# Attention in a fused sequence kernel: scores of two steps side by side, other products behind the sums, values a batch ahead, and selections on 64 partitions each

## The reference, cut to what matters

```python
qkv = x @ W_attn.T                       # 4 sets of queries, one of keys, one of values
for g in range(4):                       # query sets share keys and values
    att = einsum('bhqd,bhkd->bhqk', q_g, k) / sqrt(8)     # 16 heads of size 8, 256 tokens
    att = where(causal, att, -inf); att = softmax(att)
    outs.append(einsum('bhqk,bhkd->bhqd', att, v))
x = x + concatenate(outs) @ W_proj.T
```

## Time and profile before

| what | value |
|---|---|
| median of 3 runs | 786.8 us (785.27 to 787.71) |
| profiled execution, its own time | 785.32 us |
| its span, first to last instruction | 783.6 us |
| busy share of the span: PE, DVE, ACT, POOL | 93%, 87%, 86%, 72% |
| exponentials of attention, first and last start | 245.3 and 589.8 us |
| granted TensorE clock, mean | 0.995 |

### The profile page before, as it was taken

One profiled execution on the slowest core, in us unless ns is written; L12 is line 12 of the kernel. 1 busy time (PEld: TensorE's weight loads), 2 busy tenths in 40 slices (PEclk: granted clock), 3 DMA queues, 4 the chain that ended last, 5 costly groups with the idle time before them and its releaser, 6 DMA issues.

```text
span 783.6 us, 21138 instructions
## 1 busy us (share of the span) xinstructions
PE 730.7 (93%) x8042; PEld 410.2 (52%) x8042; DVE 678.6 (87%) x1958; ACT 671.6 (86%) x932; POOL 564.3 (72%) x622
## 2 busy tenths in 40 slices
PE   4798999999999899999999999999889999999996
PEld 3345667777776333333333333333325777677774
DVE  7998999899887878889989998878787889989885
ACT  5918999999998988888888888888976999899984
POOL 2898676665445999999999999999974445445542
PEclk9999999999999999999999999999999999999998
DMA  9210000000044244343444533554300000000000
GB/s 279 58 80 28 2 2 2 2 2 2 2 109 101 65 111 99 102 103 82 102 109 102 107 92 95 108 97 94 67 3 1 15 1 15 15 15 15 15 15 18
DMA packets 37964, 45.74 MB, mean 58 GB/s; under 512 B 6137, under 2 KB 23810, under 8 KB 37858
## 3 DMA queue, kind: packets, MB, share of 16 engines
q1 hardware_dynamic: 37858, 44.33, 23.0%
HBM read 27.53 MB, written 16.78 MB: 57 GB/s over the span
## 4 chain that ended last, share of the span: by engine, by line
PE 64%; DVE 18%; ACT 10%; issue 5%; POOL 2%; DMA 0%; ACTq 0%; DVEq 0%; POOLq 0%
PE psum L1379 15%; PE psum L1028 15%; PE psum L959 14%; PE psum L1307 7%; ACT prob L1314 6%; DVE mixed L1047 4%; PE psum L1447 4%; PE psum L1182 3%; ACT hidden_first L973 1%; ACT hidden_parts_first L975 1%; PE psum L698 1%; PE psum L1249 1%; DVE normed L394 1%; DVE stats L374 1%; DVE o_tok L1389 1%
## 5 line engine op out<-in xcount | busy, mean ns | idle before, releaser
L1314 ACT ACTIVATE prob<-psum 128x1280 f32<-128x1280 f32 x256 | 299.2, 1241 | 46.5 <-PE psum L1307 46.5
L1323 POOL TENSOR_SCALAR_AFFINE_SELECT prob<-prob 128x768 f32<-128x768 f32 (+1 forms) x384 | 311.3, 847 | 22.2 <-ACT prob L1314 20.6
L959 PE MATMUL psum<-xt_parts,w_parts 128*128 128x512 f16 x768 | 186.6, 379 | 0.0
L1379 PE MATMUL psum<-prob,vstack 128*32 128x512 f32 (+1 forms) x1536 | 167.0, 533 | 5.1 <-DVE o_tok L1389 2.2
L989 POOL TENSOR_TENSOR hidden_parts_second<-hidden_second,hidden_parts_second 128x512 f16<-128x512 f32 x64 | 77.6, 1213 | 94.8 <-ACT hidden_parts_second L975 94.8
L1047 DVE SCALAR_TENSOR_TENSOR mixed<-psum,comb_y,mixed 128x128 f32<-128x128 f32 x512 | 143.2, 340 | 1.6 <-PE psum L1028 1.5
L989 POOL TENSOR_TENSOR hidden_parts_first<-hidden_first,hidden_parts_first 128x512 f16<-128x512 f32 x64 | 79.2, 1238 | 73.0 <-ACT hidden_parts_first L975 73.0
L1307 PE MATMUL psum<-qstack,kstack 32*64 32x512 f16 (+1 forms) x1536 | 100.0, 362 | 14.8 <-ACT prob L1314 13.3
L959 PEld LDWEIGHTS psum<-xt_parts,w_parts 128*128 128x128 f16 x768 | 70.9, 98 | 65.0 <-issue 1.4
L973 ACT ACTIVATE hidden_second<-psum,b 128x512 f32<-128x512 f32 x128 | 88.4, 691 | 16.4 <-PE psum L959 14.9
L1028 PEld LDWEIGHTS psum<-w_parts,hidden_parts_first 128*128 128x128 f16 x1536 | 90.3, 98 | 19.6 <-issue 6.7
(11 more groups left out here) (155 smaller groups left out, 880.3 us busy)
## 6 DMA issues: line engine op xcount, KB each, us to landing
qstack<-qk_parts SPq DMA_DIRECT2D x128, 128.0 KB, 3.5
qk_parts<-parts SPq DMA_DIRECT2D x64, 192.0 KB, 3.2
kstack<-qk_parts SPq DMA_DIRECT2D x128, 32.0 KB, 3.5
stream<-u_folded SPq DMA_DIRECT2D x4, 512.0 KB, 7.8
kept_x<-stream SPq DMA_DIRECT2D x4, 512.0 KB, 2.7
out<-mixed SPq DMA_DIRECT2D x7, 256.0 KB, 2.3
w_whole<-L_ffn_W SPq DMA_DIRECT2D x1, 1024.0 KB, 9.0
taps<-c_taps SPq DMA_DIRECT2D x1, 640.0 KB, 6.9
```

What stands on the lines that cost most here:

```text
L959: last = e.matmul(bank(u % 4), m.w1[:, w_part, ex, cols], xt_parts[:, s, x_part, :], start=(n == 0), stop=(n == len(PRODUCTS) - 1))
L1314: e.activation(prob[:, n % PROBS, 0:COLS], psum[:, TILE * (n % 2):TILE * (n % 2) + COLS], ACT.Exp, scale=SCALE)\
L1323: return e.affine_select(kept, kept, [[0, n] for n in kept.shape[1:-1]] + [[sign, BLK]], ALU.is_ge, 0.0, base=BLK * half, channel_multipli ...
L1379: last = e.matmul(to[SLOT * lane:SLOT * (lane + 1)], vstack[:, b % 2, kind, c * LANES + lane].rearrange("p h r -> p (h r)"), weights_of(q, ...
```

## The change

- PE's order of a step becomes scores, sums, then what stands beside.
- The places beside move: queries and keys to 4, 11 and 15; the values of batch b+1 to step 7 of batch b; the projections to 7 and 15 (10 and 14 stay in the last batch). So two steps' scores stand next to each other wherever no sum and nothing beside is between them. Projections take the last 128 columns of bank 6, clear of the values' 384. The waits follow the new order of bank 6.
- Each selection takes its half's 64 partitions; both stand one behind the other at the step whose exponential they need, and the wait between them is gone (count `masked` goes by two per mask).
- POOL's reciprocal root moves from step 8 to step 6. It waits until the selections ahead of it are complete, and in step 7 the second selection waits until the root is complete.

```diff
 def tensor_at_x(e, b):
-        else:
-            e.wait_ge(v_copied, max(1, b - 1))
+        elif b == 3:
+            e.wait_ge(lo_done, 3 * b)
+        elif b > 3:
+            e.wait_ge(attn_done, HALVES * (b - 3))
+        else:
+            e.wait_ge(v_copied, 1)
 def tensor_qk(e, b, j):
-        elif j == 2 and b >= 3:
+        elif j == 1 and b == 2:
+            e.wait_ge(v_copied, b)
+        elif j == 1 and b > 2:
             e.wait_ge(attn_done, HALVES * (b - 3) + 1)
 def vector_qk_high(e, b, j):
+        elif j == 2 and b > 2:
+            e.wait_ge(projected, HALVES * (b - 2))
 def tensor_v(e, b):
-        elif b == 1:
-            e.wait_ge(lo_done, 3 * (b + 2))
+        elif b + 1 < BATCH:
+            e.wait_ge(lo_done, 3 * (b + 1) + 1)
         else:
-            e.wait_ge(attn_done, HALVES * (b - 1))
+            e.wait_ge(attn_done, HALVES * (b - 2))
 def vector_v(e, b):
         if b >= 2:
+            e.wait_ge(projected, HALVES * (b - 2) + 1)
             e.wait_ge(weighed, SUMS_B * (b - 1))
...
+    def mask_place(m, rows):          # as before, of the partitions in rows
+    def gpsimd_half_mask(e, m, half):
+        kept, sign = mask_place(m, slice(BLK * half, BLK * (half + 1))), 1 if half else -1
+        e.affine_select(kept, kept, [[0, n] for n in kept.shape[1:-1]] + [[sign, BLK]], ALU.is_ge, 0.0, base=0,
+                        channel_multiplier=-sign).then_inc(masked, 1)
     def gpsimd_mask(e, n):
         q, t = divmod(n, 4)
-        m = MASKS_Q * q
-        if t == 0:
-            gpsimd_second_half_mask(e, m)
-            if q:
-                gpsimd_first_half_mask(e, m - 1)
-        elif t == 1:
-            gpsimd_second_half_mask(e, m + 1)
-            gpsimd_first_half_mask(e, m)
-            gpsimd_first_half_mask(e, m + 1)
-        elif t == 3:
-            gpsimd_second_half_mask(e, m + 2)
+        if t != 2:
+            e.wait_ge(exped, n + 1)
+            gpsimd_half_mask(e, MASKS_Q * q + t - t // 2, 0)
+            if n == 0:
+                e.wait_ge(low_second, EXPERTS * FFN_CHUNKS)
+            elif n % STEPS_B == 7 and (root := root_of(n // STEPS_B)):
+                e.wait_ge(root[0].rstd, root[1] + 1)
+            gpsimd_half_mask(e, MASKS_Q * q + t - t // 2, 1)
...
+    QK_AT = (4, 11, 15)
+    def projects_at(b):
+        return (7, 15) if b + 1 < BATCH else (10, 14)
     def tensor_beside(e, b, at):
-        if b and at == 0:
-            tensor_v(e, b)
-        if b + 2 < BATCH and at in (4, 8, 12):
-            tensor_qk(e, b + 2, at // 4 - 1)
-        if b and at in (10, 14):
-            tensor_project(e, b - 1, at // 14)
+        if b + 2 < BATCH and at in QK_AT:
+            tensor_qk(e, b + 2, QK_AT.index(at))
+        if b + 1 < BATCH and at == 7:
+            tensor_v(e, b + 1)
+        if b and at in projects_at(b):
+            tensor_project(e, b - 1, projects_at(b).index(at))
         if b + 1 == BATCH and at == 2:
-            e.wait_ge(v_copied, BATCH)
+            e.wait_ge(attn_done, HALVES * (b - 1))
             tensor_xt(e, second, 0)
 def tensor_attention(e):
                 tensor_scores(e, n)
-            tensor_beside(e, *STARTS[n])
             if n >= 4:
                 for kind in (SUMS_Q if n < (BATCH - 2) * STEPS_B else SUMS_LAST)[n % 4]:
                     tensor_weigh(e, n // 4 - 1, kind)
+            tensor_beside(e, *STARTS[n])
 def gpsimd_attention(e):
-            if at == 8 and b % 2 == 0 and b // 2 + 2 < FFN_CHUNKS:
+            if at == 6 and root_of(b):
+                e.wait_ge(masked, HALVES * MASKS_Q * (n // 4) + HALVES * 2)
+            if at == 6 and b % 2 == 0 and b // 2 + 2 < FFN_CHUNKS:
                 gpsimd_mixed_rstd(e, b // 2 + 2)
```

More of the change, by code:

```diff
@@ L341, in build_in @@
     s_stack = [sem(f"stack_landed{i}") for i in range(2)]
-    scored, exped, half_masked, masked, weighed = (sem(n) for n in (
-        "scored", "exped", "second_half_masked", "masked", "weighed"))
+    scored, exped, masked, weighed = (sem(n) for n in (
+        "scored", "exped", "masked", "weighed"))
     turned, inverted_den, o_normed, rows_up, in_count, projected, attn_done = (sem(n) for n in (
@@ L1315, in scalar_exp @@
          .then_inc(exped, 1)
[L1319 to L1326, removed]
+    def mask_place(m, rows):
         q, t = divmod(m, MASKS_Q)
@@ L1329, in mask_place, with root_of @@
         if t < 2:
[L1330 to L1340, removed]
+            return prob[rows, slot].rearrange("p (n l g q) -> p n l g q", n=3, l=2, q=BLK)[:, :, 0]
+        return prob[rows, slot:slot + 2, 2 * BANK:COLS].rearrange("p n (g q) -> p n g q", q=BLK)
+    def gpsimd_half_mask(e, m, half):
+        kept, sign = mask_place(m, slice(BLK * half, BLK * (half + 1))), 1 if half else -1
+        e.affine_select(kept, kept, [[0, n] for n in kept.shape[1:-1]] + [[sign, BLK]], ALU.is_ge, 0.0, base=0,
+                        channel_multiplier=-sign).then_inc(masked, 1)
+    def root_of(b):
+        if b % 2 == 0 and b // 2 + 2 < FFN_CHUNKS:
+            return mixed_norm, b // 2 + 2
+        if b % 2 and b >= 3:
+            return expert_norm, second.at + (b - 3) // 2
     def gpsimd_mask(e, n):
         q, t = divmod(n, 4)
[L1345 to L1355 removed]
+        if t != 2:
[6 more added lines that the diff above has]
+            gpsimd_half_mask(e, MASKS_Q * q + t - t // 2, 1)
     def weights_of(q, kind, lane):
@@ L1426, in vector_bounds, with project_place @@
                                    op1=ALU.mult).then_inc(in_count, 1)
-    def project_bank(b):
-        return bank(6) if b + 1 < BATCH else bank(7)
+    def project_place(b, h):
+        if b + 1 == BATCH:
+            return bank(7)[:, h * P:(h + 1) * P]
+        return bank(6)[:, 3 * P:4 * P]
     def tensor_project(e, b, h):
         e.wait_ge(rows_up, HALVES * b + h + 1)
-        if b + 3 < BATCH:
-            e.wait_ge(lo_done, 3 * (b + 3) + h + 2)
+        if b + 3 < BATCH and h == 0:
+            e.wait_ge(lo_done, 3 * (b + 3) + 1)
+        elif b + 3 < BATCH:
+            e.wait_ge(lo_done, 3 * (b + 3) + 2)
         elif b + 3 == BATCH and h == 0:
-            e.wait_ge(v_copied, BATCH - 1)
+            e.wait_ge(attn_done, HALVES * b)
         elif b + 3 == BATCH:
@@ L1446, in tensor_project @@
         for g in range(SETS):
-            last = e.matmul(project_bank(b)[:, h * P:(h + 1) * P], o_rows[:, 1 - h, g, :], wproj[:, g, :],
+            last = e.matmul(project_place(b, h), o_rows[:, 1 - h, g, :], wproj[:, g, :],
                             start=(g == 0), stop=(g == SETS - 1))
@@ L1882, in vector_beside @@
     def vector_beside(e, b, at):
-        if b and at == 0:
-            vector_v(e, b)
         if b + 2 < BATCH and at == 2:
@@ L1887, in vector_beside @@
             vector_at_x_low(e, b + 2)
-        if b + 2 < BATCH and at in (4, 8, 12):
-            vector_qk_high(e, b + 2, at // 4 - 1)
-            vector_qk_low(e, b + 2, at // 4 - 1)
+        if b + 2 < BATCH and at in QK_AT:
+            vector_qk_high(e, b + 2, QK_AT.index(at))
+            vector_qk_low(e, b + 2, QK_AT.index(at))
+        if b + 1 < BATCH and at == 7:
+            vector_v(e, b + 1)
         if b and at == 5:
@@ L1894, in vector_beside @@
             vector_bounds(e, b // BOUNDED - 1, at // 13)
-        if b and at in (10, 14):
-            vector_attended(e, b - 1, at // 14)
+        if b and at in projects_at(b):
+            vector_attended(e, b - 1, projects_at(b).index(at))
         if b % 2 == 0 and b // 2 + 2 < FFN_CHUNKS:
```

10 lines of the change are left out of this document (5 added, 5 removed).

## The result

The changed kernel takes 804.9 us (median of 4 runs, 804.33 to 807.36), the kernel before, run beside it, 786.5 (785.27 to 787.71): a ratio of 1.0251, with a 95% interval of 1.0229 to 1.0273. I had forecast 778.4 with a range of 774 to 785, so it lies outside and on the other side. The profiled execution spans 805.6 us at a mean granted clock of 0.991; the run of 804.33 us had 0.995, the same as the profiled execution of the kernel before, so the clock is not what differs. Attention has taken the whole loss: from its first exponential to its last it is 362.4 us after and 344.5 before, 17.9 more.

The account below looks back on a forecast made before the run. In attention PE bounds the long quads, ACT's loop of 5.15 us the short ones. Thirteen batches gain 0.54 each (7.0), the last two 1.4: 8.4 off 785.3 gives 776.9, plus 1.5 for the median 778.4; range 774 to 785.

Parts of the forecast that it names:

- Selections: POOL's 24 mask selections a batch: no saving from half the partitions, 0.812 us each, so POOL needs 20.8 a batch.
- The slower rival: A selection on 64 partitions costs more than on 128, 5% more giving batches of 21.8 and 791 us; chance 0.10.
- Halves overlap: POOL takes both halves of a mask in the time of one, some 11 us a batch; 777 us, chance 0.15.
- The waits of POOL for itself: Two new waits on POOL, at the root and behind it: 0.15 us each, 0.3 a batch.
- Scores side by side: On PE, a pair of score blocks takes 0.52, saving 0.16; with work moved, a batch takes 20.74 us, 0.60 less.
- The neighbours forecast without a row: On PE, LATE followed by V or queries without scores between: taken as 0.57 us, give or take 0.16.
- the second quad: Steps 6 to 9 on PE, with V and a projection: 5.29 us, over the floor of 5.15.
- POOL is the bound: POOL needs 21.1 us a batch if self-waits cost 0.3 and the root's delay stays; 782.3 us, chance 0.20.
- DVE just fits: DVE's queue at step 7, 19.1 us a batch in all: LATE of step 11 ends 5.3 after step 7's, just enough.
- Waits and DMAs: nothing: SP's sends start some 4 us later, but the data is needed a whole batch (20.8) behind: no cost.
- The sum: Gain over attention: 13 batches x 0.54 = 7.0 us, batch 0 nothing, last two batches 1.4; in all 8.4.

Follow-up runs that it names:

- e11: e1 with the second selection of each quad's first mask cut to a third of its columns; 777.1 us, 0.9889 of the kernel before.
- e1: The changed kernel with POOL's part taken back (128 partitions, wait between a mask's two selections, root at step 8); 784.8 us, 0.9984 of the kernel before.
- e10: e1 with DVE's statistics in attention taken of only one tile in four; 784.8 us, 0.9976 of the kernel before.
- e7: e1 with DVE's statistics moved from step 1 to step 6 of each batch; 788.9 us, 1.0044 of the kernel before.
- the two probes: Two kernels, each executed once, of only groups of 16 POOL instructions, varying partitions, halves and operations; selections 0.86 us apart, 0.97 with halves in turn.

## Why the prediction was wrong

The step that failed is *Selections*: "So I take no saving and 0.812. The bounds are 0.41 ... and 0.85". In the changed kernel one takes 0.913, above the upper bound too, 0.10 over the value taken, and 24 of them make 2.4 us a batch. The question that I asked (what do fewer partitions cost?) I answered rightly: nothing, 0.86 on 128, 64 and 32. I didn't ask what it costs to go back and forth between them, since each row of before stands among neighbours on the same partitions. The price then went through by the prediction's own working, with 0.97 for the root in place of 1.3 for root and waits, in a queue that was already at 20.5 of 21.34: 22.9 a batch.

- *The slower rival* named the right place and the right sign of the outcome (24 selections pass 21.34 from 0.835 on), but for a cost of 64 partitions that doesn't exist, and at 5% where 12% came; 791 against 804.9. Its mark (a mean distance over 0.83) was the first thing to show.
- *Halves overlap* was wrong, and turned round: disjoint halves overlap less than equal ones.
- *The waits of POOL for itself*, put at 0.15 each, were too dear: the root and what follows it take 0.97 after and before, so the wait behind it costs nothing that can be seen; the one ahead of it is at most the 0.08 from the recorded end of the selection to the root.
- *Scores side by side* held. The neighbours forecast without a row measure LATE to V 0.57, V 0.73, projection 1.09, as taken; the pair ahead of the double sum takes 0.45, not 0.52, and by that alone the second quad is 5.22 and not 5.29. e11, with POOL relieved, has the quads 5.15, 5.22, 5.15, 5.15.
- *POOL is the bound* (782.3, chance 0.20) is the rival nearest to e1, the change without the halves: 784.8. I had let 20.80 stand since "those selections are done some 0.6 before LATE". e11 against e1 measures 7.8 us for relief on POOL. A reason can be argued and isn't shown: POOL was 20.5 of work in 21.34, a batch of 20.74 leaves it little slack to make up a delay, and batches that have one (up to 22.1) keep it. But e1's undisturbed batch of 21.15 loses its time at a wait for DVE and not for POOL.
- *DVE just fits* held for the time and not for the waits: with its work cut (e10) it is 784.8 as in e1, but in e1 the queries of step 4 wait for it, seven times and 3.5 us in all between 300 and 500 us, and the prediction had no wait there. It also took DVE's 19.1 us a batch as fixed, where e1 and e11 differ by 7 in 100 us for the same instructions.
- *Waits and DMAs: nothing* was wrong as put. The prediction had the data needed a whole batch behind, but didn't ask how much of it the sends take: in e10 SP's sends of one batch run from 397.92 to 413.77, 15.9 us, and the last lands some 3 later, so about 2 of a batch are left. That shows as waits at the start of some batches, 4.9 us in e1, whose worth is open.
- *The sum*, 8.4 us, is near what e11 gains (785.7 to 777.1, 8.7), but e11 leaves out work, and the nearness is partly luck, since the parts differ: from the first exponential to the last it gains 7.9, of which 12 batches have 0.43 each and the last three 2.7, where 13 x 0.54 and 1.4 were taken.

## What to carry to other kernels

Count not only what an instruction costs, but what stands ahead of it: on GpSimd, keep instructions on the same partitions together, and measure from start to start. An engine that is at 96% of the time before becomes the bound of any gain elsewhere; ask first what it would need at the new time. To find which of two late engines matters, take work from each alone and from both, and look whether the cut also made the other engine's instructions shorter, as e11's did: a wait that moved from one place to another (e7) said nothing.

## What the runs showed of the hardware

On GpSimd an instruction whose first partition is another than that of the one ahead (in all cases here it had no partition in common with it either) starts about 0.1 us later: selections of 768 columns 0.97 in place of 0.86, of 512 columns 0.72 in place of 0.61, subtractions 1.33 for 1.22, memsets 0.57 for 0.47, scalings 1.56 for 1.45. A change in the number of partitions alone costs nothing (128 and 0 to 63 in turn, 0.86). Without counting a semaphore the selections in turns start 0.95 apart, so the count isn't the cause. The groups of the two probes, subtractions on one half (of the first), then in turns, and scalings in turns and on one half (of the second):

```profile
151.44 19.55 POOL L67 TENSOR_TENSOR made<-buf,other 64x512 f32<-64x512 f32 x16
```

```profile
99.74 21.23 POOL L55 TENSOR_TENSOR made<-buf,other 64x512 f32<-64x512 f32 x16
...
151.65 24.94 POOL L67 TENSOR_SCALAR made<-buf 64x512 f32<-64x512 f32 x16
176.67 23.28 POOL L70 TENSOR_SCALAR made<-buf 64x512 f32<-64x512 f32 x16
```

The number of partitions is no cost either way: 0.86 on 32, 64 and 128. On VectorE a normalisation of 256 columns from two SBUF inputs is recorded with a median of 0.46 us in e11 and of 0.87 in e1, where GpSimd has 2.0 us more to do in a batch; what makes it longer, no run isolates. On TensorE the second of two blocks of scores side by side is cheap (0.52 for two ahead of the sum of LATE, 0.45 ahead of the double sum, 0.33 to 0.34 for one), but only while ScalarE has freed its place by then.
